# Three turns of the identity behind the sums of each step of layer 0's edge loop, from step 19 on

## The chip, the cores and the metric

The kernel runs on one core of one Trainium2 chip. The metric is the device time of one execution in microseconds, from the runs of the program; the median of three runs before the change is 929.86 us (928.89 to 931.95).

## The reference, cut to what matters

A graph of 1,250 nodes with 512 features and 21,250 edges (each edge both ways, and a loop per node, sorted by destination) goes through two layers. In each, every edge makes a message from its source node's row and its own features, and the messages are summed by destination. The part that the change touches is in layer 0:

```python
src, dst = (edge_index[0], edge_index[1])
msg = jax.nn.relu(x[src] + edge_attr @ W_e + b_e)
aggr = jax.ops.segment_sum(msg, dst, num_segments=x.shape[0])
h = (1.0 + eps) * x + aggr
h = jax.nn.silu(_bn(h @ W1 + b1, g1, beta1))
h = h @ W2 + b2
return jax.nn.silu(_bn(h, g2, beta2))
```

Layer 0 is followed by x = layernorm(x + layer 0), and then by layer 1, whose messages are `relu(h[src] @ .. + edge_attr @ .. + b1)` summed in the same way and then put through a gated unit. All is in float32.

## The kernel before, in words

The program is written by hand, engine by engine; each engine has its own list of instructions in program order, and they meet by semaphores only. Nothing reorders them.

Edges come in tiles of 128 (`TILES` = 167, E = 21,250). The edge loop, `edges(L)`, is run once per layer, in steps of two tiles (`STEPS` = 84), numbered j. Twelve tiles make a group with one window of 128 destination nodes; so a window lasts six steps. The parts of a step, by engine:

- GpSimd gathers the source rows of a tile into one of 14 slots by an indirect DMA (`gather`, L479). It waits until the slot's old tile is done with.
- ScalarE copies the gathered rows of odd tiles into a PSUM bank (`place`, L895), so that TensorE adds onto them; it makes the high half of each message (relu, L939), and the high half of the features of each chunk of four tiles (L895).
- VectorE adds the product to the gathered rows for even tiles (`add_product`, L1170), makes the low half of a message (L1162; not for every fourth tile, which is kept whole), the low features (L1085), and the one-hot matrices that say which destination an edge has (L1156).
- TensorE makes the edge products of the step's two tiles (`edge_product`, L577, two products a tile in layer 0, three in layer 1), and then the sums of the two tiles of two steps ago (`sum_product`): one-hot times message, as a high and a low product (L607, L608) or, for the whole tile, in one line that is two passes (L605).
- SyncE loads the features, four tiles at a time.

When a group's last sums are in, ScalarE copies the window's sums out of PSUM (`copy_window`, L895 with tile `sums`), in step last + 2; TensorE turns them with four transposes (`turn_window`, L630), at the end of step last + 3; VectorE adds them to the nodes' rows (`add_window`, L1185).

TensorE's order within a step is that of the code: edge products, sums, then `turn_x` (L643) in steps 3 to 12 of layer 0, then `turn_window` where a group ends. `turn_x` puts x, four transposes per block of 128 nodes, into bank 7 (`start_bank`), from where ScalarE starts the sums. In step 14 TensorE counts, in the same bank, the edges that lie outside their window (L655), and in step 16 VectorE makes a flag of the count (`left_flag`) and tells it by `flag_ready`. From there on bank 7 is not used in layer 0.

`keep_busy(turns)` (L557) transposes the identity so many times; it stands before the edge loops and around the steps between the two layers, not in the edge loop.

Of the kernel before, what the change touches and what calls it, by code (L numbers as in the profile page):

```python
# [11 lines left out]
P = 128  # L12
# [14 lines left out]
STEPS = -(-TILES // 2)  # L27
BLOCKS = -(-N // P)
# [9 lines left out]
TURN_X = 3  # L38
# [11 lines left out]

LAST_PIECES = [(0, P), (P, 3 * P), (4 * P, 3 * P), (7 * P, N - 7 * P)]
HEAD = 2
KA = KD - 1

COLS = {}
# [22 lines left out]
def gnn_program(nc, x, src, dst, attr0, attr1, W_e, b_e, W1, W2, V1h, V1e, v_b1, V2, v_b2, Wg, cols, out):  # L78
    with ExitStack() as ctx:
# [16 lines left out]
        def keep(name, width, dt=F32, parts=P):  # L96
            t = at(name, [parts, width], dt, small[0])
            small[0] += -(-width * 4 // 64) * 64
            assert small[0] <= A0, name
            return t  # L100
# [7 lines left out]
        ident = keep("ident", P)  # L108
# [119 lines left out]
        start_bank = bank[7]  # L228
# [9 lines left out]
        left_ready, left_counted, flag_ready = map(sem, ("left_ready", "left_counted", "flag_ready"))  # L238
# [73 lines left out]
        def step_tiles(j):  # L312

            return range(2 * j, min(TILES, 2 * j + 2))
# [6 lines left out]
        def last_step(g):  # L321

            return (min(TILES, (g + 1) * GROUP) - 1) // 2
# [220 lines left out]
        def _(pe):  # L544
# [9 lines left out]
            def keep_busy(turns):  # L554

                for _ in range(turns):
                    nc.tensor.transpose(bank[3][:, 0:P], ident[:, :], ident[:, :])  # L557

            def edge_product(L, t):

                i, c, ks = t // 2, t // CHUNK, slice(t % CHUNK * P, (t % CHUNK + 1) * P)
                if t % CHUNK == 0:
                    pe.wait_ge(attr_split[L], c + 1)
                if odd(t):

                    pe.wait_ge(placed[L], i + 1)
                else:

                    wait(pe, added[L], i - ADD_BANKS + 1)
                if L == 0:  # L570

                    passes = [(attr_1[:, c % RING, ks], We_hi[:, :]), (attr_hl[:, c % RING, ks], We_lh[:, :])]
                else:
                    hi, lo = attr_hi[:, c % RING, ks], attr_lo[:, c % RING, ks]
                    passes = [(hi, V1e_hi[:, :]), (hi, V1e_lo[:, :]), (lo, V1e_hi[:, :])]
                for n, (features, W) in enumerate(passes):
                    mm = nc.tensor.matmul(edge_bank(t), features, W, start=n == 0 and not odd(t),  # L577
                                          stop=n == len(passes) - 1, skip_group_check=odd(t))
                mm.then_inc(add_mm[L], 1)

            def prime(L):

                anything = (We_hi[0:1, :], x1_hi[0:1, 0, 0:D])[L]
                for b in place_bank:
                    mm = nc.tensor.matmul(b, ones_row[:, :], anything, start=True, stop=True)
                mm.then_inc(primed[L], 1)
                if L == 0:
                    keep_busy(12)

            def sum_product(L, t):  # L590

                g, c = t // GROUP, t // CHUNK
                start, stop = t % GROUP == 0, t % GROUP == GROUP - 1 or t == TILES - 1
                if whole(L, t):
                    pe.wait_ge(relued[L], t + 1)
                else:
                    pe.wait_ge(low[L], lows(L, t + 1))
                if t % CHUNK == 0:
                    pe.wait_ge(hot_ready[L], c + 1)
                if start:  # L600

                    wait(pe, window_added[L], g - 1)
                acc, h = sum_bank[g % 2], hot[L][:, c % HOT, t % CHUNK, :]
                if whole(L, t):
                    mm = nc.tensor.matmul(acc, h.bitcast(F32), msg_whole[:, t % MSG, :], start=start, stop=stop)  # L605
                else:
                    nc.tensor.matmul(acc, h, msg_hi[L][:, t % MSG, :], start=start, stop=False)  # L607
                    mm = nc.tensor.matmul(acc, h, msg_lo[L][:, t % MSG, :], start=False, stop=stop)  # L608
                if L == 1 and t == chunk_tiles(c).stop - 1:
                    mm = degrees(c)  # L610
                mm.then_inc(summed[L], 1)
# [13 lines left out]
            def turn_window(L, g):  # L625


                pe.wait_ge(window_copied[L], g + 1)
                for k in range(KD):
                    tr = nc.tensor.transpose(sum_bank[g % 2][:, k * P:(k + 1) * P], sums[L][:, g % 2, k * P:(k + 1) * P],  # L630
                                             ident[:, :])
                tr.then_inc(window_turned[L], 1)

            def turn_x(b):

                pe.wait_ge(x_in_done[b // XB], 16)
                if b == 0:
                    pe.wait_ge(base_copied, 1)
                else:

                    pe.wait_ge(agg_start, b)
                for k in range(KD):
                    tr = nc.tensor.transpose(start_bank[:, k * P:(k + 1) * P], x_in[:, b, k * P:(k + 1) * P], ident[:, :])  # L643
                tr.then_inc(x_turned, 1)

            def edges(L):
                prime(L)
                for j in range(STEPS + SUM_LAG + TURN_AFTER):
                    if j < STEPS:
                        for t in step_tiles(j):  # L650
                            edge_product(L, t)
                    if L == 0 and j == TURN_X + BLOCKS + 1:
                        pe.wait_ge(left_ready, 1)
                        pe.wait_ge(agg_start, BLOCKS)
                        nc.tensor.matmul(misc[0:1, 16:17], left_n[:, 0:1], ones[:, 0:1], start=True,  # L655
                                         stop=True).then_inc(left_counted, 1)
                    if 0 <= j - SUM_LAG < STEPS:
                        for t in step_tiles(j - SUM_LAG):
                            sum_product(L, t)
                    if L == 0 and 0 <= j - TURN_X < BLOCKS:  # L660
                        turn_x(j - TURN_X)
                    for g in range(GROUPS):
                        if last_step(g) + SUM_LAG + TURN_AFTER == j:
                            turn_window(L, g)
# [42 lines left out]
            keep_busy(24)  # L707
            pe.wait_ge(we_split, 1)
            edges(0)
            keep_busy(20)  # L710
            leftover(0)
# [34 lines left out]
            def turn_y(t, ks):  # L746

                r = rows_in(t)
                for k in ks:
                    tr = nc.tensor.transpose(bank[t % 2][0:r, k * P:(k + 1) * P], y_t[:, k, t * P:t * P + r], ident[:, :])  # L750
                return tr


            pe.wait_ge(silu_done, KH + KD - 1)
            for t in range(HEAD):
                turn_y(t, range(KA)).then_inc(head_turned, 1)
            pe.wait_ge(mlp_out, 3 * (KH + KD))
            keep_busy(16)
            for t in range(BLOCKS + 3):
                if t < BLOCKS:  # L760
                    for i, (at_node, _) in enumerate(LAST_PIECES):
                        if t == at_node // P:

                            pe.wait_ge(silu_done, KH + KD + i)
                    if t < HEAD:

                        pe.wait_ge(head_added, t + 1)
                        turn_y(t, [KA]).then_inc(back_turned, 1)
                        keep_busy(8)
# [28 lines left out]

            pe.wait_ge(v1e_split, 1)
            edges(1)  # L800
            leftover(1)

# [271 lines left out]
        def _(dve):  # L1074
# [259 lines left out]
            def head_add(t, cols):  # L1334

                if cols.start == 0:
                    if t == 0:
                        dve.wait_ge(rows_in_done, 32)
                    dve.wait_ge(head_turned, t + 1)
                else:  # L1340
                    dve.wait_ge(back_turned, t + 1)
                return nc.vector.tensor_tensor(lnx[:, t, cols], bank[t][:, cols], rows[:, t, cols], ALU.add)
# [4 lines left out]
            for c in range(KH + KD):  # L1347
# [9 lines left out]
                if c == KH + KD - 1:  # L1357

                    head_add(0, slice(0, KA * P)).then_inc(head_added, 1)
                if c + W1_FIRST < KH:  # L1360
# [47 lines left out]

            early, late = slice(0, KA * P), slice(KA * P, D)
            for t in range(BLOCKS + 3):  # L1410
                if t < HEAD:

# [192 lines left out]
```

## Time and profile before

| what | value |
|---|---|
| median of three runs | 929.86 us (928.89 to 931.95) |
| the profiled execution's own time | 934.32 us |
| its span, first to last instruction | 932.5 us |
| its mean granted TensorE clock | 0.938 |
| busy share of TensorE, VectorE, ScalarE, GpSimd | 88%, 69%, 48%, 39% |
| layer 0's edge loop, about | 14 to 278 us |
| layer 1's edge loop, about | 439 to 725 us |

Times in the profile are from the span's start. PE is TensorE's matmuls (transposes too), PEld its weight loads, DVE is VectorE, ACT ScalarE, POOL GpSimd. A line such as L577 is a line of the kernel before. PEclk is the granted clock: 1.00 is 2.4 GHz and 0.50 is 1.2 GHz. A wait is put down to whoever ended it: "issue" is a wait that nothing in the profile explains, "remote" one that was ended by a source that the profile can't name. The starts of matmuls are recorded; their ends are modelled, so durations of neighbours overlap, and the distance from start to start is the better measure.

### The profile page before, as it was taken

What the parts mean: (1) busy time and instruction counts of PE and PEld (TensorE: products, weight loads), DVE (VectorE), ACT (ScalarE), POOL (GpSimd) and SP (SyncE); (2) the same over time, 40 slices, a digit from 0 to 9 for tenths busy, and PEclk for the clock granted to TensorE, in tenths of its full rate; (3) what the DMA queues carried; (4) which work ended last, traced back from release to release, by engine and by line L of the source; (5) the groups of instructions that cost most, each with busy time, mean ns of one, the idle gap of its engine ahead of it and who ended that gap; (6) DMA issues with size and microseconds to landing.
All of it is one profiled execution on the core that took longest, in us unless ns stands there. A gap on an engine that the chain in (4) does not pass through costs nothing.

```text
span 932.5 us, 11516 instructions
## 1 busy us (share of the span) xinstructions
PE 820.9 (88%) x3754; PEld 666.7 (71%) x3754; DVE 639.3 (69%) x1138; ACT 452.1 (48%) x810; POOL 362.4 (39%) x379
## 2 busy tenths in 40 slices
PE   7797868888799999997678989989789999999996
PEld 6464645555568999875467767767668889898995
DVE  6687757777698954396377868878689666354345
ACT  4696756776676422211365656656556321111122
POOL 6576656666620000024656656656552000000001
PEclk9899888889899999999789999989989999999998
DMA  8988776577640050015757766667652111010011
GB/s 226 289 267 252 226 216 205 179 215 214 205 146 25 1 181 1 1 46 171 214 157 233 222 208 212 200 198 216 202 180 80 35 69 68 1 68 1 1 46 65
DMA packets 49814, 133.87 MB, mean 144 GB/s; under 512 B 8815, under 2 KB 9071, under 8 KB 49368
## 3 DMA queue, kind: packets, MB, share of 16 engines
q0 software_dynamic: 26560, 87.05, 30.4%
q1 hardware_dynamic: 22700, 45.60, 15.3%
q8 instruction: 31, 0.51, 0.2%
q10 hardware_dynamic: 492, 0.45, 0.2%
q14 instruction: 31, 0.25, 0.1%
HBM read 127.95 MB, written 5.12 MB: 143 GB/s over the span
## 4 chain that ended last, share of the span: by engine, by line
PE 64%; DVE 17%; issue 7%; another core or an unknown queue 7%; ACT 2%; DMA 1%; DVEq 0%; ACTq 0%; POOL 0%; POOLq 0%
PE banks L550 35%; PE banks L577 14%; DVE msg_lo L1162 6%; PE banks L607 5%; DVE raw L1170 5%; PE banks L608 4%; PE banks L605 2%; PE banks L630 2%; PE banks L621 1%; DVE hot L1156 1%; DVE attr_hl L1085 1%; DVE agg L1185 1%; DVE attr_lo L1085 1%; DVE stats L1298 1%
## 5 line engine op out<-in xcount | busy, mean ns | idle before, releaser
L479 POOL DMA_INDIRECT raw<-table_dram,src_sb x166 | 166.7, 1004 | 108.0 <-DVE msg_lo L1162 57.6
L479 POOL DMA_INDIRECT raw<-in_x,src_sb x166 | 168.0, 1012 | 93.3 <-issue 46.1
L1170 DVE TENSOR_TENSOR raw<-banks,raw 128x512 f32<-128x512 f32 x168 | 115.4, 687 | 116.8 <-remote 71.5
L939 ACT ACTIVATE msg_hi<-raw 128x512 fp32r<-128x512 f32 x168 | 105.8, 630 | 130.9 <-DVE raw L1170 83.3
L607 PE MATMUL banks<-msg_hi,hot 128*128 128x512 f32 x293 | 126.5, 432 | 35.4 <-DVE msg_lo L1162 32.2
L501 POOL TENSOR_TENSOR moments<-moments,minus_half 128x1 f32<-128x1 f32 x32 | 20.2, 630 | 306.0 <-DVE moments L1304 280.4
L608 PE MATMUL banks<-msg_lo,hot 128*128 128x512 f32 x293 | 120.3, 411 | 0.0
L1162 DVE SCALAR_TENSOR_TENSOR msg_lo<-raw,msg_hi 128x512 fp32r<-128x512 f32 x168 | 114.6, 682 | 0.0
L895 ACT ACTIVATE banks<-raw 128x512 f32<-128x512 f32 x166 | 98.7, 595 | 18.1 <-DMA raw<-table_dram,src_sb 11.6
L607 PEld LDWEIGHTS banks<-msg_hi,hot 128*128 128x128 f32 x293 | 58.6, 200 | 65.2 <-DVE msg_lo L1162 47.7
L577 PE MATMUL banks<-We_hi,attr 97*128 97x512 f32 x167 | 91.6, 548 | 3.5 <-issue 2.8
L1162 DVE SCALAR_TENSOR_TENSOR msg_lo<-banks,msg_hi 128x512 fp32r<-128x512 f32 x125 | 85.3, 683 | 0.0
L577 PE MATMUL banks<-V1e_hi,attr_hi 128*128 128x512 f32 x167 | 73.9, 442 | 9.2 <-ACT banks L895 6.7
L939 ACT ACTIVATE msg_hi<-banks 128x512 fp32r<-128x512 f32 x125 | 72.9, 583 | 8.6 <-remote 6.4
L577 PE MATMUL banks<-We_lh,attr_hl 128*128 128x512 f32 x167 | 71.6, 429 | 0.0
L577 PE MATMUL banks<-V1e_lo,attr_hi 128*128 128x512 f32 x167 | 69.5, 416 | 0.0
L577 PE MATMUL banks<-V1e_hi,attr_lo 128*128 128x512 f32 x167 | 69.3, 415 | 0.0
L608 PEld LDWEIGHTS banks<-msg_lo,hot 128*128 128x128 f32 x293 | 58.8, 201 | 11.2
L1156 DVE TENSOR_TENSOR hot<-iota_f,in_window 128x512 fp32r<-128x512 f32 x84 | 56.9, 678 | 0.0
L630 PE MATMUL banks<-ident,sums 128*128 128x128 f32 x112 | 22.3, 333 | 36.5 <-issue 19.9
L577 PEld LDWEIGHTS banks<-We_hi,attr 97*128 97x128 f32 x167 | 35.2, 211 | 25.9 <-issue 17.5
L550 PE MATMUL banks<-x_hi,Wg_hi 128*128 128x512 f32 (+2 forms) x144 | 50.7, 352 | 0.5 <-issue 0.5
(169 smaller groups left out, 1772.6 us busy)
## 6 DMA issues: line engine op xcount, KB each, us to landing
attr_sb<-in_attr SPq DMA_DIRECT2D x84, 128.0 KB
attr_sb<-in_attr SPq DMA_DIRECT2D x42, 256.0 KB
Wg_raw<-in_Wg SPq DMA_DIRECT2D x3, 1536.0 KB, 6.3
raw<-in_x,src_sb POOLq DMA_INDIRECT x166
raw<-table_dram,src_sb POOLq DMA_INDIRECT x166
x_in<-in_x SPq DMA_DIRECT2D x5, 512.0 KB
rows<-in_x SPq DMA_DIRECT2D x1, 2560.0 KB, 12.2
table_dram<-table_sb SPq DMA_DIRECT2D x9, 256.0 KB, 2.0
```

What stands on the lines that cost most here:

```text
L479: pool.indirect_dma_start(rows_of(L, t), None, tables[L], bass.IndirectOffsetOnAxis(ap=src_sb[:, t:t + 1], axis=0)).then_inc(gathered[t % ...
L501: nc.gpsimd.tensor_tensor(moments[:, slot * 4 + 2:slot * 4 + 3], moments[:, slot * 4 + 1:slot * 4 + 2], minus_half[:, 0:1], ALU.pow).then_ ...
L550: mm = nc.tensor.matmul(acc, a, b, start=start and i == 0, stop=stop and i == len(passes) - 1)
L577: mm = nc.tensor.matmul(edge_bank(t), features, W, start=n == 0 and not odd(t), stop=n == len(passes) - 1, skip_group_check=odd(t))
L607: nc.tensor.matmul(acc, h, msg_hi[L][:, t % MSG, :], start=start, stop=False)
L608: mm = nc.tensor.matmul(acc, h, msg_lo[L][:, t % MSG, :], start=False, stop=stop)
L630: tr = nc.tensor.transpose(sum_bank[g % 2][:, k * P:(k + 1) * P], sums[L][:, g % 2, k * P:(k + 1) * P], ident[:, :])
L895: return nc.scalar.activation(to, of, ACT.Copy)
L939: nc.scalar.activation(to[:, t % MSG, :], edge_bank(t) if odd(t) else rows_of(L, t), ACT.Relu).then_inc(relued[L], 1)
L1156: nc.vector.tensor_tensor(hot[L][:, c % HOT, 0:len(tiles), :], nodes, own, ALU.is_equal).then_inc(hot_ready[L], 1)
L1162: nc.vector.scalar_tensor_tensor(msg_lo[L][:, t % MSG, :], edge_bank(t) if odd(t) else rows_of(L, t), 0.0, msg_hi[L][:, t % MSG, :].bitcas ...
L1170: nc.vector.tensor_tensor(rows_of(L, t), edge_bank(t), rows_of(L, t), ALU.add).then_inc(added[L], 1)
```

## The change

Behind the sums of each step of layer 0 with TURN_X + BLOCKS + 5 < j < STEPS, that is 18 < j < 84, so steps 19 to 83, TensorE waits for `flag_ready` and transposes the identity three times into the first 128 columns of bank 7. Nobody reads them.

```diff
--- before.py
+++ after.py
@@ -50,6 +50,7 @@
 
 LAST_PIECES = [(0, P), (P, 3 * P), (4 * P, 3 * P), (7 * P, N - 7 * P)]
 HEAD = 2
+FILL = 3
 KA = KD - 1
 
 COLS = {}
@@ -659,6 +660,10 @@
                             sum_product(L, t)
                     if L == 0 and 0 <= j - TURN_X < BLOCKS:
                         turn_x(j - TURN_X)
+                    if L == 0 and TURN_X + BLOCKS + 5 < j < STEPS:
+                        pe.wait_ge(flag_ready, 1)
+                        for _ in range(FILL):
+                            nc.tensor.transpose(start_bank[:, 0:P], ident[:, :], ident[:, :])
                     for g in range(GROUPS):
                         if last_step(g) + SUM_LAG + TURN_AFTER == j:
                             turn_window(L, g)
```

On TensorE the order changes at each step's end. Here is step 20, which ends with the turn of a window, as it stood in the kernel before (L577 are the edge products, L607 and L608 the sums, L630 the turn of the window; `sums_104` is ScalarE's copy of it, `hot_102` the one-hots):

```order
L577 MATMUL banks<-We_hi,attr_111 128x512 [waits added0,attr_split0]
L577 MATMUL banks<-We_lh,attr_hl 128x512
L577 MATMUL banks<-We_hi,attr_111 128x512 [waits placed0]
L577 MATMUL banks<-We_lh,attr_hl 128x512
L607 MATMUL banks<-msg_hi_97,hot_102 128x512 [waits window_added0,hot_ready0,low0]
L608 MATMUL banks<-msg_lo_100,hot_102 128x512
L607 MATMUL banks<-msg_hi_97,hot_102 128x512 [waits low0]
L608 MATMUL banks<-msg_lo_100,hot_102 128x512
L630 MATMUL banks<-ident,sums_104 128x128 [waits window_copied0]
L630 MATMUL banks<-ident,sums_104 128x128 x3
```

And step 20 in the changed kernel, where the lines have a number higher by one:

```order
L578 MATMUL banks<-We_hi,attr_111 128x512 [waits added0,attr_split0]
L578 MATMUL banks<-We_lh,attr_hl 128x512
L578 MATMUL banks<-We_hi,attr_111 128x512 [waits placed0]
L578 MATMUL banks<-We_lh,attr_hl 128x512
L608 MATMUL banks<-msg_hi_97,hot_102 128x512 [waits window_added0,hot_ready0,low0]
L609 MATMUL banks<-msg_lo_100,hot_102 128x512
L608 MATMUL banks<-msg_hi_97,hot_102 128x512 [waits low0]
L609 MATMUL banks<-msg_lo_100,hot_102 128x512
L666 MATMUL banks<-ident 128x128 [waits flag_ready]
L666 MATMUL banks<-ident 128x128 x2
L631 MATMUL banks<-ident,sums_104 128x128 [waits window_copied0]
L631 MATMUL banks<-ident,sums_104 128x128 x3
```

Three transposes of the identity (L666) stand behind the step's sums and ahead of the turn of the window. In a step without a turn they are its last instructions. Nothing else moved, on this engine or another.

## Rows read from the trace of the kernel before

**Rows 1.** The page: busy time of the engines, and the chain that ended last.

```profile
PE 820.9 (88%) x3754; PEld 666.7 (71%) x3754; DVE 639.3 (69%) x1138; ACT 452.1 (48%) x810; POOL 362.4 (39%) x379
...
PE 64%; DVE 17%; issue 7%; another core or an unknown queue 7%; ACT 2%; DMA 1%; DVEq 0%; ACTq 0%; POOL 0%; POOLq 0%
```

**Rows 2.** Table by stretches: us, busy us (count) of each engine, PEclk, DMA share, GB/s.

```profile
34.00:70.71 36.71, 33.91 (x149) 23.53 (x147) 30.41 (x52) 32.63 (x63) 25.80 (x25) 0.98 0.87 272
76.39:268.77 192.38, 158.75 (x541) 108.44 (x540) 144.03 (x229) 136.28 (x261) 119.27 (x119) 0.88 0.69 206
520.45:711.84 191.39, 167.23 (x750) 132.54 (x748) 151.34 (x257) 117.76 (x216) 116.30 (x116) 0.94 0.65 200
101.73:105.36 3.63, 3.63 (x11) 2.53 (x9) 3.48 (x6) 1.95 (x5) 1.68 (x2) 0.50 0.20 65
108.51:112.65 4.14, 4.14 (x18) 3.03 (x17) 4.08 (x8) 3.71 (x8) 3.17 (x3) 1.00 0.79 234
```

**Rows 3.** Groups by form, TensorE: late part of layer 0; then layer 1; then early part.

```profile
L577 PE MATMUL banks<-We_hi,attr 97*128 97x512 f32 x124 | 70.1, 565 | 0.9 <-ACT banks L895 0.5 <-issue 0.3
...
L630 PE MATMUL banks<-ident,sums 128*128 128x128 f32 x44 | 9.8, 362 | 19.0 <-issue 15.0 <-ACT sums L895 4.0
...
L577 PE MATMUL banks<-V1e_hi,attr_hi 128*128 128x512 f32 x119 | 51.7, 434 | 0.0
...
L643 PE MATMUL banks<-ident,x_in 128*128 128x128 f32 x34 | 5.4, 282 | 0.2 <-issue 0.2
L630 PE MATMUL banks<-ident,sums 128*128 128x128 f32 x8 | 1.3, 279 | 0.4 <-issue 0.4
```

**Rows 4.** Timeline of TensorE, a smooth stretch: start us, us, what [idle before].

```profile
108.51 0.40 PE L577 MATMUL banks<-We_hi,attr 97*128 97x512 f32 x1
108.74 0.40 PE L577 MATMUL banks<-We_lh,attr_hl 128*128 128x512 f32 x1
...
112.65 0.40 PE L577 MATMUL banks<-We_hi,attr 97*128 97x512 f32 x1
```

**Rows 5.** Timeline of TensorE, the turn of a window and the step behind it.

```profile
116.55 0.40 PE L608 MATMUL banks<-msg_lo,hot 128*128 128x512 f32 x1
120.89 1.12 PE L630 MATMUL banks<-ident,sums 128*128 128x128 f32 x4 [3.94 <-issue]
...
122.24 0.63 PE L577 MATMUL banks<-We_lh,attr_hl 128*128 128x512 f32 x1
122.66 0.63 PE L577 MATMUL banks<-We_hi,attr 97*128 97x512 f32 x1
```

**Rows 6.** Timeline of ScalarE at the same turn.

```profile
120.24 0.60 ACT L895 ACTIVATE sums<-banks 128x512 f32<-128x512 f32 x1 [4.03 <-remote]
```

**Rows 7.** Who waited for whom, late part of layer 0: us, times, longest.

```profile
DVE raw L1170 <- remote: 30.5, 8, 4.8
...
ACT sums L895 <- remote: 18.5, 6, 4.0
```

**Rows 8.** Timeline of TensorE in the early part: a step with four transposes.

```profile
37.42 0.48 PE L577 MATMUL banks<-We_hi,attr 97*128 97x512 f32 x1
...
39.38 0.60 PE L643 MATMUL banks<-ident,x_in 128*128 128x128 f32 x4
39.73 0.48 PE L577 MATMUL banks<-We_hi,attr 97*128 97x512 f32 x1
```

**Rows 9.** Timeline of TensorE at the kernel's start, at the lower clock.

```profile
11.38 2.56 PE L557 MATMUL banks<-ident 128*128 128x128 f32 x12
```

**Rows 10.** Timeline of TensorE in layer 1: the first products of two pairs of steps.

```profile
643.16 0.39 PE L577 MATMUL banks<-V1e_hi,attr_hi 128*128 128x512 f32 x1
...
648.14 0.39 PE L577 MATMUL banks<-V1e_hi,attr_hi 128*128 128x512 f32 x1
```

**Rows 11.** Timeline of GpSimd in the late part of layer 0: one gather.

```profile
115.52 0.95 POOL L479 DMA_INDIRECT raw<-in_x,src_sb  x1 [0.30 <-issue]
```

**Rows 12.** Who waited for whom, layer 1: us, times, longest.

```profile
ACT sums L895 <- remote: 18.4, 5, 5.0
```

## The prediction

> **What bounds the kernel now.** Start with the page. TensorE is busy for 88% of the span and heads the chain of work that ended last with 64% [rows 1]. The change touches only the edge loop of layer 0, from step 19 on, so the shares of the whole span say little; I cut that stretch out. The table by stretches has three rows [rows 2]: the early part of layer 0 (34.00 to 70.71 us), its late part (76.39 to 268.77), and most of layer 1's edge loop (520.45 to 711.84). In the late part the mean granted clock is 0.88, against 0.98 and 0.94 in the others, and VectorE, ScalarE and GpSimd are busy for 75, 71 and 62% of it: nothing is full on average. The groups by form count 124 first products there, two per step, so 62 steps in 192.38 us, **3.10 us a step** [rows 3].
>
> The timeline of TensorE shows what a step is when nothing stands still. From 108.51 to 112.65 its instructions start 0.23 to 0.24 us apart without a gap, two steps in 4.14 us [rows 4]: 2.07 us a step. So in a smooth stretch TensorE itself is on the path. VectorE is close behind: it is busy for 4.08 of those 4.14 us [rows 2]. Eleven turns of a window (44 transposes [rows 3]) add 0.43 us each (priced below), 0.08 a step. The smooth step is then 2.15 us, and 3.10 less 2.15 leaves **0.95 us a step, 59 us in all, that is lost**.
>
> Where it is lost: TensorE's timeline at the turn of a window [rows 5]. It ends its sums at 116.95 and stands still until 120.89; ScalarE, whose copy of the window it waits for, is itself released after 4.03 us, by a source that the profile can't name ("remote") [rows 6]. Such standstills come about once a window: ScalarE's copy alone waited 18.5 us in 6 of them, VectorE's add 30.5 us in 8, up to 4.8 at a time [rows 7]. After each the clock stands at 0.50: the stretch from 101.73 to 105.36 is one step of 3.63 us, all of it TensorE's [rows 2]. So two losses: the standstill and the slow clock behind it. The mean clock of 0.88 over 192.38 us means 23 us of full-speed cycles missing, or 46 us at the lower level (1.2 GHz), some of them in standstills. Half of 46 us, 23 us, is the most that a clock held at 2.4 GHz could give back.
>
> **The change, part by part.** It adds three transposes of the identity, with their loads, behind the sums of steps 19 to 83: 65 steps, 195 transposes. It removes and moves nothing. No engine waits for them and their bank is free by then.
>
> *The wait* on the flag adds no time: VectorE sets it in step 16, three steps earlier, and it stays set. Behind it are only TensorE's own instructions.
>
> *One transpose, full clock.* TensorE already does almost this: in the early part each step ends with four transposes of x. Its step from 37.42 to 39.73 takes 2.31 us, and eight products at 0.235 would take 1.88, so four transposes cost 0.43: 0.35 from the first of them (39.38) to the next product (39.73), and 0.08 that the first product behind transposes takes longer [rows 8]. Three cost 0.35 x 3/4 + 0.08: **0.345 us a step**.
>
> *At the lower level:* twelve turns of the identity at the kernel's start take 2.56 us, 0.213 each, against 0.35 / 4 = 0.088 above [rows 9]; three take 0.64 us. With 46 us at that level and some 3.3 us to a slow step, about 14 steps pay 0.30 us more: 4 us.
>
> *Sum with all losses as they are:* 65 x 0.345 = 22.4, plus 4, less what falls into a standstill. In a turning step the three transposes stand behind the sums and ahead of the turn, where TensorE waits anyway: 11 x 0.345 = 4 us covered. That is **+22 us**, the upper bound.
>
> *What the losses do.* The trace has no row for this stage with fill in it, so I bound it by the two other stretches. Layer 1: 119 first products, 59 steps in 191.39 us [rows 3], 3.24 a step; its smooth pace is 4.98 us for two steps (643.16 to 648.14) [rows 10], with the turns 2.57; lost: 0.67. The early part: 13 steps (counted by their first products) in 36.7 us, 2.82 each; 42 transposes make ten and a half sets of four, 0.35 a step, so smooth 2.42; lost: 0.40. A step that gives TensorE more to do loses less. One reason is in the rows: GpSimd starts a gather every 1.25 us while it is not held (0.95 and 0.30 between two) [rows 11], 2.50 us for a step's two, so a TensorE at 2.07 runs faster than rows are fetched, and one at 2.5 doesn't. With the fill the smooth step is 2.15 + 0.345 = 2.50 us. By layer 1's losses it would be 3.17 in all: 0.07 more than now, **+4 us** over 65 steps. Layer 1 is nearest in pace, the stage's own losses are nearest in everything else (copies, adds, loads); I take the middle, **+13 us**, since the losses plainly don't vanish at a pace of 2.57.
>
> The sum is made against the profiled execution, 934.32 us (span 932.5): 947. The median of the runs is 929.86, 4.5 lower, so the forecast against it is **943 us**. A measurement of this kernel can tell about 0.3%, 2.8 us, from no change.
>
> **The rivals.**
>
> *A: the fill takes the standstills away (faster).* Place: the waits of ScalarE's copy and VectorE's add in steps 19 to 74. For it: the early part has four transposes in most steps, a clock of 0.98, and no standstill of that kind; it lost only 0.40 a step. Price: 2.50 + 0.40 = 2.90 us, 0.20 less than now, 65 x 0.20 = 13 us: 917. It decides once a standstill falls from some 4 us to under about 2.5. Against it: layer 1 goes at 2.57 and still has ScalarE's copy waiting 18.4 us in 5 [rows 12]; and in the early part ScalarE had the turned x to copy as well, which the fill doesn't give it.
>
> *B: only the clock is kept up (no difference).* The drops follow standstills of 3 to 4 us. If the added columns held the clock at 2.4 GHz behind them, the 14 slow steps would each give back some 1.3 us (3.3 us against 2.07), 18 in all, and the fill would cost 18 (22 less the 4 for slow steps): 930, with 925 as the end where all 23 us come back. Against it: the fill is issued ahead of the standstill and is over within 0.35 us, and nothing is in TensorE's queue during the 3.94 us [rows 5]; what the clock falls for is missing there. The Trainium skill, "TensorE: Matmul & The Clock Gate", section "HAM oscillation — how this bites in real kernels", says that waits for data let TensorE drop to its lower clock, once per wait, and that the remedy is to order the work so that it meets no such waits. The trace agrees with the first half: the 3.94 us at 116.95 are followed by products 0.43 us apart [rows 5]. By that rule work added beside the waits helps only so far as it shortens them.
>
> *C: VectorE and ScalarE are set back too (slower still).* A later product delays VectorE's add and the gathers behind it, so each standstill stays and the slow steps lengthen: the 4 us aren't covered, and losses grow by a tenth (6 us): +32, 961.
>
> *D: it does nothing to the path.* If VectorE at 4.08 of 4.14 us were the true bound, 0.345 a step would need slack in TensorE; the rows show none in smooth steps [rows 4]. It can hide only where TensorE waits. I count D with B.
>
> **How the numbers follow.** Forecast (+4 to +22 us): 0.56. A 0.22, B with D 0.14, C 0.08. The range: the forecast's own bounds give 934 to 952; it has to reach past A (917, give or take a few) on the low side and part of C on the high side: **911 to 956**. The likeliest case's own range stands at 934 to 952. Both signs hold weight. Slower by over 0.3%: the forecast and C, 0.61. Within: most of B, 0.13. Faster: A and the rest of B, 0.26.
>
> **What would show it.** Right: the late part of layer 0 grows from 192 to some 205 us, smooth pairs of steps take 4.8 us in place of 4.14, standstills ahead of the turns still number about ten, somewhat shorter, the mean clock stays near 0.88, layer 1 and the dense products keep their length. Wrong: smooth pairs at 4.14 with the transposes in gaps (D); "remote" waits of ScalarE's copy and VectorE's add well under 10 us in all (A); a clock above 0.95 with standstills as long as before (B).

## The result, and the profile after

| | before | changed |
|---|---|---|
| median of 20 runs, us | 930.73 (918.54 to 936.58) | 933.68 (926.01 to 942.59) |
| ratio, 95% interval | | 1.0063 (1.0039 to 1.0087) |
| the profiled execution: its own time / span, us | 934.32 / 932.5 | 930.32 / 928.5 |

The change makes the kernel slower by 0.6%, some 6 us, where 13 were forecast. The medians of all twenty runs lie only 3 us apart; the ratio is that of the faster runs, those within 1.5% of their own kernel's fastest (15 of 20 before, 19 of 20 after). So the sign is clear and the size is not: 3 to 6 us. The two profiled executions happen to lie the other way round by 4 us: single executions of this kernel scatter by more than the effect, so only stretches of the two traces are compared below, and the verdict is that of the runs.

The page of the changed kernel: the span, the engines' busy time, the chain that ended last.

```profile
span 928.5 us, 11906 instructions
...
PE 827.1 (89%) x3949; PEld 678.4 (73%) x3949; DVE 638.7 (69%) x1138; ACT 451.9 (49%) x810; POOL 361.2 (39%) x379
...
PE 67%; DVE 18%; another core or an unknown queue 6%; issue 6%; ACT 1%; DMA 1%; DVEq 0%; ACTq 0%; POOL 0%; POOLq 0%
```

The table by stretches of the changed kernel (us; busy us and count of PE, PEld, DVE, ACT, POOL; PEclk; DMA share; GB/s): the late part, 62 steps as in [rows 2]; one step behind a standstill; two smooth steps.

```profile
72.84:267.94 195.10, 169.83 (x727) 121.64 (x726) 144.54 (x230) 136.37 (x262) 120.69 (x120) 0.92 0.70 209
165.41:169.12 3.71, 3.71 (x14) 2.66 (x12) 3.09 (x5) 2.85 (x7) 2.79 (x4) 0.67 0.71 209
169.12:173.91 4.79, 4.79 (x25) 3.58 (x24) 2.40 (x5) 2.57 (x5) 3.37 (x4) 1.00 0.79 237
```

The same 62 steps took 192.38 us before and take 195.10 now, 3.10 and 3.15 a step. The granted clock rose from 0.88 to 0.92. TensorE's groups by form there:

```profile
L578 PE MATMUL banks<-We_hi,attr 97*128 97x512 f32 x124 | 57.5, 464 | 0.1
...
L608 PE MATMUL banks<-msg_hi,hot 128*128 128x512 f32 x93 | 42.2, 454 | 25.1 <-DVE msg_lo L1167 25.1
...
L666 PE MATMUL banks<-ident 128*128 128x128 f32 x186 | 32.1, 284 | 0.0
...
L631 PE MATMUL banks<-ident,sums 128*128 128x128 f32 x44 | 6.8, 278 | 0.0
```

All 186 turns of those steps are there, and no idle time stands before them. The idle time in front of the turn of a window, 19.0 us before [rows 3], is gone; 25.1 us now stand before the high product of the sums (L608). TensorE's timeline, two smooth steps:

```profile
169.12 0.48 PE L578 MATMUL banks<-We_hi,attr 97*128 97x512 f32 x1
...
170.85 0.39 PE L609 MATMUL banks<-msg_lo,hot 128*128 128x512 f32 x1
171.08 0.49 PE L666 MATMUL banks<-ident 128*128 128x128 f32 x3
171.32 0.48 PE L578 MATMUL banks<-We_hi,attr 97*128 97x512 f32 x1
...
172.81 1.02 PE L606 MATMUL banks<-msg_whole,hot 128*128 128x512 f32 x2
173.67 0.49 PE L666 MATMUL banks<-ident 128*128 128x128 f32 x3
173.91 0.48 PE L578 MATMUL banks<-We_hi,attr 97*128 97x512 f32 x1
```

The first takes 2.20 us, the second, with a whole tile, 2.59: **2.39 us a step**, 2.07 before [rows 4]. So the turns stand on the path at 0.32 us a step, close to the 0.345 worked out. Now a standstill and the slow step behind it, from TensorE's timeline and, last, VectorE's; then who waited for whom in the late part (us, times, longest), the changed kernel and one row of the kernel before:

```profile
155.03 0.60 PE L631 MATMUL banks<-ident,sums 128*128 128x128 f32 x4
...
158.75 0.40 PE L578 MATMUL banks<-We_lh,attr_hl 128*128 128x512 f32 x1
163.04 0.80 PE L608 MATMUL banks<-msg_hi,hot 128*128 128x512 f32 x1 [3.89 <-DVE msg_lo L1167]
...
164.49 0.63 PE L609 MATMUL banks<-msg_lo,hot 128*128 128x512 f32 x1
164.91 0.84 PE L666 MATMUL banks<-ident 128*128 128x128 f32 x3
165.41 0.78 PE L578 MATMUL banks<-We_hi,attr 97*128 97x512 f32 x1
```

```profile
161.10 0.69 DVE L1190 TENSOR_TENSOR agg<-banks,agg 128x512 f32 x1 [5.22 <-remote]
```

```profile
PE banks L608 <- DVE msg_lo L1167: 25.1, 11, 3.9
...
DVE agg L1190 <- remote: 21.0, 5, 5.2
...
DVE raw L1175 <- remote: 7.4, 4, 3.8
```

```profile
DVE agg L1185 <- remote: 8.5, 2, 6.0
```

TensorE waits 3.89 us for a message that VectorE could not begin, because VectorE itself was held, in its add of a window (L1190), by a source that the profile can't name (the last section comes back to it). Such waits of ScalarE and VectorE come to 28.4 us in 9 in the late part, where the kernel before had 57.5 us in 16: the 49.0 of [rows 7] and 8.5 in the add of a window (some of that at the same time). So the turns are paid in full in every step, 62 x 0.32 = 20 us, and the stretch grows by 2.7: most of their price comes back as waits, and slow steps behind them, that don't happen. Smooth pace with the turns of windows 2.39 + 0.07 = 2.46; 3.15 less 2.46 leaves **0.69 us a step lost, 0.95 before**, and layer 1 lost 0.67 at its pace.

### The profile page after: what moved, and what is told of

It reads as the page before. It is cut to its first block, busy times and chain, and to the rows that moved or that the text cites. A ratio compares the mean times of both kernels' runs of the same rounds, so it can differ in the third digit from the quotient of the medians.

```text
span 928.5 us, 11906 instructions
## 1 busy us (share of the span) xinstructions
PE 827.1 (89%) x3949; PEld 678.4 (73%) x3949; DVE 638.7 (69%) x1138; ACT 451.9 (49%) x810; POOL 361.2 (39%) x379
## 3 DMA queue, kind: packets, MB, share of 16 engines
q0 software_dynamic: 26560, 87.05, 30.8%
## 4 chain that ended last, share of the span: by engine, by line
PE 67%; DVE 18%; another core or an unknown queue 6%; issue 6%; ACT 1%; DMA 1%; DVEq 0%; ACTq 0%; POOL 0%; POOLq 0%
PE banks L551 35%; PE banks L578 15%; DVE msg_lo L1167 7%; PE banks L608 5%; DVE raw L1175 5%; PE banks L609 5%; PE banks L606 2%; DVE hot L1161 1%; PE banks L666 1%; PE banks L622 1%; PE banks L631 1%; DVE attr_hl L1090 1%; DVE attr_lo L1090 1%; DVE agg L1190 1%
## 5 line engine op out<-in xcount | busy, mean ns | idle before, releaser
L608 PE MATMUL banks<-msg_hi,hot 128*128 128x512 f32 x293 | 126.3, 431 | 44.4 <-DVE msg_lo L1167 42.3
L608 PEld LDWEIGHTS banks<-msg_hi,hot 128*128 128x128 f32 x293 | 58.7, 200 | 72.6 <-DVE msg_lo L1167 55.4
L578 PE MATMUL banks<-We_hi,attr 97*128 97x512 f32 x167 | 78.2, 468 | 3.1 <-issue 2.9
L578 PE MATMUL banks<-We_lh,attr_hl 128*128 128x512 f32 x167 | 68.7, 412 | 0.0
L551 PE MATMUL banks<-x_hi,Wg_lo 128*128 128x512 f32 (+2 forms) x144 | 50.8, 353 | 0.0
L551 PE MATMUL banks<-x_lo,Wg_hi 128*128 128x512 f32 (+2 forms) x144 | 50.8, 353 | 0.0
```

Source lines behind the costliest of these rows:

```text
L551: mm = nc.tensor.matmul(acc, a, b, start=start and i == 0, stop=stop and i == len(passes) - 1)
```

## Experiments: more turns, and no gathers

A *standstill* is a stretch of some microseconds in which TensorE does nothing; the *smooth pace* is the time of a step without one, with its share of a window's turn. Each set of runs below met one chip, and every kernel in it is compared with the kernel before on the same chip. Theory S: with its standstills the late part of layer 0 is held to some 3.1 us a step by something outside TensorE, and work added to an engine only takes the place of standstills until its own pace reaches that. Theory P, the one of the forecast: the losses shrink only partly as the pace falls. The edits, each one alone; first the number of turns, on the changed kernel:

```diff
-FILL = 3
+FILL = 6
```

and likewise 12. Six turns:

> Six turns a step in place of three; steps 19 to 83 of layer 0 took 200.1 us before and 200.0 us with three. Theory S (those steps are held to about 3.08 us a step by something outside TensorE, of which the standstills are the visible part, so that more work on TensorE only takes their place): the smooth step grows to 2.74 us and the 65 steps still take 200 to 205 us; the whole stays within 0.5% of the kernel with three. Theory P (TensorE's work is paid in full, and the losses per step merely fall with the pace, from 0.95 to about 0.7 us): 65 x 0.345 more, less a little, so the steps take 215 to 222 us and the whole is 1.6 to 2.4% over the kernel before.

Twelve turns:

> Twelve turns a step. The smooth step is 2.07 + 12 x 0.088 + 0.08 + 0.08 for the turn of a window = 3.29 us, over the 3.08 that the steps take on average now. Theory S: TensorE becomes the bound at last, few or no standstills are left, the clock stays full, 65 steps take 214 to 220 us: 1.5 to 2.2% over before. Theory P: losses of 0.4 to 0.7 us a step on top, 240 to 260 us, 4 to 6.5% over before.

Then the gathers of layer 0 from the fifteenth tile on were left out. What layer 0 adds up is then made from what already stands in the fourteen slots; every instruction of the other engines stays. On the kernel before:

```diff
+        told = sem("told")
...
-                before = L * len(range(t % RAW, TILES - 1, RAW))
-                engine.wait_ge(gathered[t % RAW], (before + t // RAW + 1) * 16)
+                if L == 0 and t >= RAW:
+                    engine.wait_ge(told, t - RAW + 1)
+                else:
+                    engine.wait_ge(gathered[t % RAW], (L + t // RAW + 1) * 16)
...
+                if L == 0 and t >= RAW:
+                    nc.gpsimd.nop().then_inc(told, 1)
+                    return
                 pool.indirect_dma_start(rows_of(L, t), None, tables[L],
```

> The kernel before with the gathers of layer 0 from tile 14 on left out (GpSimd only tells that the slot is ready, so its rows are those of an earlier tile). If the standstills come from the gathers (theory S with the gathers as the supply), steps 19 to 83 run at the smooth pace of 2.15 us with the clock at 1.00: 140 us in place of 200, the whole about 870 us, 6% under. If the standstills come from the exchange between the engines itself (sums, copy of the window, turn), they stay, and the steps take 190 to 200 us.

The same on the changed kernel:

> The changed kernel (three turns a step) with the same gathers left out. With the standstills gone nothing covers the turns: 65 x 0.345 = 22 us over the run without gathers and without turns under theory S and under theory P alike, if the smooth step is TensorE's; if VectorE (4.08 of 4.14 us busy) is the bound there, clearly less than 22.

Measured in one set, against a kernel before of 937.18 us:

| kernel | median, us | ratio to before | steps 19 to 80 in its trace, us |
|---|---|---|---|
| six turns | 945.29 | 1.0091 (1.0036 to 1.0147) | 198.29 |
| twelve turns | 961.53 | 1.0278 (1.0220 to 1.0336) | 216.12 |
| no gathers | 884.52 | 0.9443 (0.9380 to 0.9505) | 144.34 |
| no gathers, three turns | 891.54 | 0.9528 (0.9475 to 0.9581) | 153.40 |

Their rows for those 62 steps, in this order, from the tables by stretches:

```profile
75.22:273.51 198.29, 181.27 (x913) 136.39 (x912) 145.69 (x230) 138.26 (x264) 121.23 (x119) 0.98 0.69 204
```

```profile
80.44:296.56 216.12, 214.77 (x1286) 176.58 (x1284) 145.34 (x229) 137.72 (x263) 121.61 (x120) 1.00 0.63 186
```

```profile
64.87:209.21 144.34, 141.88 (x541) 94.69 (x540) 142.41 (x229) 134.46 (x261) 0.00 (x0) 1.00 0.20 57
```

```profile
69.63:223.03 153.40, 153.27 (x728) 115.81 (x726) 145.11 (x230) 135.72 (x263) 0.00 (x0) 1.00 0.18 54
```

Two smooth steps with six turns, then two pairs with twelve:

```profile
132.57:138.01 5.44, 5.44 (x32) 4.25 (x30) 3.09 (x5) 3.59 (x8) 4.22 (x5) 1.00 0.82 246
```

```profile
134.49:141.22 6.73, 6.73 (x43) 5.54 (x41) 5.58 (x9) 5.62 (x12) 4.96 (x5) 1.00 0.62 167
141.22:147.99 6.77, 6.77 (x43) 5.56 (x42) 4.32 (x7) 3.83 (x9) 3.23 (x3) 1.00 0.54 163
```

Six turns give TensorE 0.65 us more a step (5.44 / 2 less 2.07), 40 us over 62 steps, and the stretch is 6 us longer. At twelve turns the clock is 1.00, TensorE is busy for 214.77 of 216.12 us, and it has no standstill of 2 us left; only there is TensorE the bound, at 3.49 us a step. The unnamed waits are not gone even so: VectorE still has 14.7 us of them in 4, up to 4.9 at a time, which no longer reach TensorE.

```profile
DVE raw L1175 <- remote: 8.2, 2, 4.9
```

Theory S is the nearer one between 0 and 6 turns: each lands at 3.10 to 3.20 us a step. Its own figures were low, though. For 65 steps it gave 200 to 205 us with six turns, and the traces make 208; it gave 214 to 220 with twelve, and they make 227. Part of that is the price of a turn: three, six and twelve cost 0.32, 0.65 and 1.31 us a step, 0.11 each in proportion, and not 0.088 each with 0.08 once. Without gathers the standstills are all gone, without any turn: clock 1.00, 2.33 us a step. The exchange between the engines doesn't make them by itself; the gathers are needed. And in that quiet stretch the three turns cost 9.1 us, not 62 x 0.32 = 20: VectorE is busy for 142.41 of 144.34 us, so it is the bound there, and TensorE, at 2.15 with the turns of windows, has room. By the medians of the runs the three turns cost 7.0 us there. The smooth stretch that the forecast read as TensorE's own had VectorE within 2% of it, and over longer stretches VectorE decides.

## Experiments: what of a gather does it, and a delay elsewhere

Narrow gathers, on the kernel before (layer 0 then sums other numbers than the tiles' rows):

```diff
+                w = P if L == 0 and t >= RAW else D
-                pool.indirect_dma_start(rows_of(L, t), None, tables[L],
+                pool.indirect_dma_start(rows_of(L, t)[:, 0:w], None, tables[L] if w == D else x.rearrange("n (a d) -> (n a) d", d=P),
```

> The kernel before, with the gathers of layer 0 from tile 14 on a quarter as wide (128 of 512 columns; what they fetch is not the tile's rows). Each is still one indirect DMA of 128 rows with its descriptors and its sixteen signals, but a quarter of the bytes. Without any gather the 65 steps ran at 2.32 us each, with no standstill. If the bytes (the DMA engines' time) hold the steps to 3.08 us, the standstills go as they did without gathers: about 885 us, 5 to 6% under before. If it is what a gather costs whatever its width (descriptors, signals, GpSimd's 1.25 us each), the standstills stay, about one a window: within 1.5% of before.

No feature loads after the third chunk (the edges' features are then those of the first three chunks), on the kernel before:

```diff
                 wait(sp, attr_split[L], c - RING + 1)
+                if L == 0 and c >= RING:
+                    for h in range(P // parts):
+                        nc.sync.nop().then_inc(attr_in[L][c % RING], 16)
+                    return
```

> The kernel before, with the feature loads of layer 0 from the fourth chunk on left out (SyncE only tells that the chunk is there, so its values are old). The gathers stay whole. If the sum of all DMA traffic makes the standstills, a fifth less of the bytes and a third less of the packets brings them down by a third or more: the whole 1.5 to 4% under before. If it is the gathers alone, nothing changes: within 1% of before.

A delay on VectorE in place of the turns, on the kernel before:

```diff
                             low_message(L, t)
+                    if L == 0 and TURN_X + BLOCKS + 5 < j < STEPS:
+                        for _ in range(2):
+                            link(nc.vector.tensor_copy(lf_hot[0][:, :], iota_f[:, :]))
```

> The kernel before, with two small copies on VectorE in each of steps 19 to 83 in place of TensorE's turns, about 0.2 us each and 0.5 a step with what links them, 30 us of VectorE's time in all. TensorE is given no more columns. Theory S (the steps have room for any delay up to about 3.1 us a step): VectorE's own load rises from 2.3 to 2.8 us a step and the whole grows by 0 to 1.2%, as with the turns, with fewer and shorter standstills. If the small price of the three turns came from a clock that they kept up, this run has nothing of the kind and costs its 30 us, 3% over before.

This set told something else first: **the kernel before took 827.89 us** in it (824.52 to 829.88, 21 runs), 100 less than on any chip until then. Against that: narrow gathers 823.62 us, 0.9944 (0.9925 to 0.9962); no feature loads 828.39, 1.0008 (0.9989 to 1.0028); the delay 848.37, 1.0262 (1.0238 to 1.0286). In its traces the clock stands at or near 1.00 through the whole late part and the unnamed standstills are absent, so the three say nothing about them here. All three were run again; the narrow gathers and the delay then met a chip that has them. The copies' group and the table's row for 62 steps of the delay:

```profile
L1234 DVE COPY lf_hot<-iota_f 128x128 f32<-128x128 f32 x122 | 27.6, 226 | 2.1
```

```profile
67.32:240.80 173.48, 157.72 (x541) 88.14 (x540) 167.39 (x350) 136.41 (x261) 114.88 (x120) 1.00 0.80 235
```

The copies are 27.6 us of VectorE's time, and the kernel paid 20.5 for them.

## Experiments: both kinds of chip

The kernels were run again in three more sets. The first of them met a chip with standstills (before: 932.69 us):

> The kernel before, unchanged, for a trace of it on this chip. In the last set the kernel before took 828 us, in the sets ahead of it 930 to 937: the standstills are not in the program. If this chip is one of the fast ones: no idle stretch of 2 us or more at TensorE in steps 19 to 83, the clock at 1.00, and those steps in 155 to 170 us (GpSimd's two gathers at 1.25 us each, 2.50 a step, being the bound: 162). If it is one of the slow ones: the trace looks as the first did.

> The changed kernel. On a chip without standstills: if GpSimd's 2.50 us a step is the bound, TensorE's 2.48 us with three turns still fit beneath it and the whole is within 0.6% of before (0 to 5 us). If TensorE and VectorE at 2.1 to 2.3 us are the bound there, the turns cost 10 to 22 us, 1.2 to 2.7%. On a chip with standstills: again 0.3 to 1% over before.

> Six turns, smooth step 2.72 + 0.08 us. On a chip without standstills nothing is left that could pay for it: 65 x (2.80 - 2.50) = 20 us over before if GpSimd's pace is the bound there, 2.4%, and 30 us or more if it is not. On a chip with standstills: about 1%, as before.

> The kernel before without the gathers of layer 0 from tile 14 on. On a chip without standstills it can only take away GpSimd's pace: 65 x (2.50 - 2.32) = 12 us less, 1.4% under before, in place of the 5.6% that it took away on the slow chip. On a chip with standstills: 5 to 6% under again.

Measured: unchanged 929.45 us, 1.0034 (0.9988 to 1.0080); three turns 932.94, 1.0050 (1.0011 to 1.0090); six turns 930.91, 1.0045 (1.0012 to 1.0078); no gathers 876.42, 0.9464 (0.9401 to 0.9526). Three and six turns can't be told apart, and hardly from no change: the unchanged kernel's own ratio reaches 1.0080, and the medians of all runs with three turns and before, 932.94 and 932.69, are the same.

The next met one with standstills too (before: 929.86 us):

> The kernel before, unchanged, for its trace on this chip. Where the runs of before are near 828 us: steps 19 to 83 in 155 to 170 us, no idle stretch of 2 us at TensorE, the clock at 1.00, layer 1's edge loop shorter by some 50 us too. Where they are near 930: as the first trace, 195 to 202 us.

> The changed kernel. Where before is near 828 us: 0 to 5 us over it if GpSimd's 2.50 us a step is the bound there, 10 to 22 us if TensorE and VectorE are. Where before is near 930 us: 0.3 to 0.8% over it, the third time.

> The kernel before with gathers of 128 columns in place of 512 in layer 0 from tile 14 on. Where before is near 930 us: if the bytes make the standstills, 5 to 6% under before, as without gathers; if what each gather costs whatever its width makes them, within 1.5%. Where before is near 828 us: 0.3 to 1% under before, as it was.

> The kernel before with two small copies more on VectorE in steps 19 to 83, 0.3 us a step or more. They cost 20 us, 2.6%, on the chip without standstills. Where before is near 930 us: 0 to 1% if any delay is taken up by the standstills, whichever engine has it; 2 to 2.6% if only TensorE's own work is.

Measured: unchanged 930.29 us, 1.0002 (0.9969 to 1.0036); three turns 937.67, 1.0104 (1.0054 to 1.0153); narrow gathers 927.17, 0.9941 (0.9900 to 0.9983); the delay 938.13, 1.0101 (1.0043 to 1.0159). Three turns cost more here than the 0.3 to 0.8% expected. The late part in all traces of chips with standstills:

| kernel | 62 steps, us | unnamed waits of ScalarE and VectorE, us (times) | TensorE idle for 2 us or more, times |
|---|---|---|---|
| unchanged | 192.38, 194.65, 196.49 | 57.5 (16), 61.1 (20), 56.4 (17) | 8, 10, 9 |
| three turns | 195.10, 199.12, 202.51 | 28.4 (9), 27.9 (8), 33.1 (8) | 5, 6, 8 |
| six turns | 198.29, 200.15 | 20.3 (9), 23.0 (10) | 3, 3 |
| twelve turns | 216.12 | 14.7 (4) | 0 |
| delay on VectorE | 200.53 | 39.1 (14) | 8 |
| narrow gathers | 190.10 | 36.5 (16) | 7 |

So the sum isn't quite constant: 3.10 to 3.17 us a step without turns, 3.15 to 3.27 with three, 3.20 and 3.23 with six. Narrow gathers in the table by stretches, and VectorE's unnamed wait there:

```profile
70.72:260.82 190.10, 157.24 (x541) 106.53 (x540) 144.28 (x229) 136.49 (x261) 119.34 (x120) 0.89 0.30 85
```

```profile
DVE raw L1171 <- remote: 19.8, 9, 4.7
```

A quarter of the gathers' bytes, DMA share down from 0.69 to 0.30, and VectorE's add still waits 19.8 us in 9 for the unnamed source, at a clock of 0.89; the kernel gains 0.6% (0.2 to 1.0), as on the chip without standstills. The packets fell too, from 80 to 32 a gather by the page's counts (26,560 in all before, 19,264 with 152 of 332 gathers narrow). The unnamed waits are as many as before and a third shorter in all (36.5 us in 16 against 56.4 in 17 on this chip), so bytes or packets have a part in it, but a small one in the time: 6 us of the 50 that go without gathers. The rest is something that a gather brings with it at either width. The delay on VectorE, 2.6% where there are no standstills, costs 1.0% here:

```profile
73.36:273.89 200.53, 164.71 (x541) 97.09 (x540) 167.36 (x350) 137.60 (x261) 114.96 (x120) 0.93 0.69 203
```

So about half of a delay on VectorE is taken up: 9 us are paid (4 to 15) in place of 20.5. Here TensorE was given no work that could hold its clock up, and the clock is still 0.93, against 0.87 for the unchanged kernel on this chip. The last set met a chip without standstills again (before: 827.56 us):

> The changed kernel. Where before is near 828 us, its steps take about 2.6 us each (163.6 us for 63 steps in the run without feature loads there), and TensorE with three turns needs 2.48: 0 to 5 us over before if the gathers' pace leaves room, up to 10 us, as in the pair without gathers, if it does not. Where before is near 930 us: 0.3 to 1% over it, as three times already.

> The kernel before, for its trace on this chip. Near 828 us: no standstills, steps 19 to 83 in about 165 us, layer 1's edge loop some 50 us shorter. Near 930 us: as the first trace.

> The kernel before without the feature loads of layer 0 from the fourth chunk on. Where before is near 930 us: narrow gathers took away 0.6% there, so bytes don't count; if every DMA's descriptors and signals count, the loads (two in two steps, beside four gathers) are a third of them and 1.5 to 2.5% go; if it is the gathers alone, within 0.5%. Where before is near 828 us: within 0.3%, as it was.

Measured: three turns 832.43 us, 1.0067 (1.0040 to 1.0094); unchanged 827.58, 1.0008 (0.9987 to 1.0029); no feature loads 828.64, 1.0009 (0.9990 to 1.0028). Rows for 62 steps: unchanged (and below it 59 steps of layer 1's loop, those of [rows 2]), three turns, no feature loads.

```profile
65.70:221.70 156.00, 141.96 (x541) 94.34 (x540) 145.66 (x230) 136.44 (x261) 119.17 (x120) 1.00 0.90 262
453.04:604.77 151.73, 151.73 (x749) 127.66 (x748) 151.18 (x257) 118.32 (x218) 114.49 (x118) 1.00 0.82 255
```

```profile
67.03:227.41 160.38, 157.27 (x728) 114.23 (x726) 146.46 (x230) 136.61 (x261) 123.03 (x120) 1.00 0.86 254
```

```profile
62.54:223.45 160.91, 145.20 (x541) 93.14 (x540) 146.07 (x230) 136.49 (x261) 123.23 (x122) 1.00 0.71 204
```

Without standstills the unchanged kernel takes 2.52 us a step, which is GpSimd's pace, as its timeline shows (gathers 1.25 us apart), and the gathers are what ScalarE waits for there:

```profile
98.58 0.95 POOL L479 DMA_INDIRECT raw<-in_x,src_sb  x1 [0.30 <-issue]
99.84 0.95 POOL L479 DMA_INDIRECT raw<-in_x,src_sb  x1 [0.30 <-issue]
```

```profile
ACT banks L895 <- DMA raw<-in_x,src_sb: 18.5, 23, 1.6
```

With three turns it takes 2.59 us, 4.4 us more over 62 steps; the whole grows by 4.9. (One trace's stretch is not that sharp: without feature loads it is 160.91, 4.9 more, and the whole is unchanged.)

This bears on what was said above. Three turns cost 4.9 us where there are no standstills, and 5 to 10, by the ratios of three sets, where there are: no less. With three turns the pace of the gathers alone would take up most of the price, so that the shrinking standstills are needed for it can't be told from these runs. It can be with more work. By the pace of 2.52, six turns would cost 65 x (2.79 - 2.52) = 18 us and twelve 65 x (3.45 - 2.52) = 60 (estimates, not run on such a chip); with standstills they cost 4 to 9 and 24 to 26. The delay on VectorE was run on both: 20.5 and 9 us. Layer 1's 59 steps, 191.39 us in the first trace, take 151.73, at a clock of 1.00 and with TensorE never idle: 2.57 us a step, exactly its smooth pace. Of the 102 us between the chips, 36 lie in layer 0's late part and 40 in those steps of layer 1.

## Why the forecast was right in direction and at least twice too large

- *What bounds the stretch.* The standstills and the slow clock behind them were read rightly as the loss; 0.95 us a step of it was there, but not all of it is standstills: a chip without any still takes 2.52 us a step, 0.37 over the smooth 2.15, at the gathers' pace. That the smooth step is TensorE's own was half right. VectorE is within 2% of it, and without gathers VectorE decides: three turns then cost 9 us where the sum had 20. On a chip without standstills GpSimd's 2.50 decides, and they cost 5.
- *The price of the turns.* 0.345 us a step was forecast; smooth steps grew by 0.32, and a pair of them took 4.79 us, 4.8 forecast. The flag's wait cost nothing. This term held, though its make did not: the cost is in proportion, 0.11 a turn.
- *The cover in turning steps.* 4 us were said to be hidden ahead of a turn, at all eleven turns; only seven of them had a wait ahead of them before. The idle time ahead of the turn did go, all 19 us of it, but because the standstills moved and thinned out, not by 0.345 us each.
- *What the losses do* is the step that failed. It gave +4 us by layer 1's losses and +22 by unchanged losses, and took the middle, 13, "since the losses plainly don't vanish at a pace of 2.57". They fell to 0.69, layer 1's figure almost to the hundredth, which makes +2.9 us over 65 steps in the traces; the runs say 6 (3.6 to 8.1). The upper bound's reason, that the stage's own losses are nearest in everything else, says nothing of how they change with the pace, so it should not have pulled the value up. The late part was to grow from 192 to 205 us at a clock of 0.88; it grew to 195, at 0.92. The forecast's own rows lay on both sides of 2.50, the early part at 2.42 with 0.40 and layer 1 at 2.57 with 0.67; that the second was hit so closely is in part luck. In its place the runs showed that the losses shrink by nearly all that the pace grows: they were 0.95, 0.69, 0.41 and 0.04 us a step at smooth paces of 2.15, 2.46, 2.79 and 3.45 (0, 3, 6, 12 turns). The sum stays at 3.10 to 3.20 in these traces, up to 3.27 in the others, until the pace itself passes it. Three stretches at 2.15, 2.42 and 2.57 stood in the forecast with sums of 3.10, 2.82 and 3.24. The longest two lie close together at paces far apart, which is what such a floor under the sum looks like; the early part lies under it and isn't explained by it. What sets it, and why at 3.1 to 3.3, stays open.
- *Rival A* had the mechanism, fewer standstills, but they shrank by what was added and by no more; that takes the price back and gives no gain. Its sign came true without its price: the unnamed waits of ScalarE's copy and VectorE's add fell to 7.4 us, while 21.0 stood at VectorE's add of a window, where the sign didn't look. *Rival B*: the clock did rise, to 0.92, 0.98 and 1.00 with 3, 6 and 12 turns. It rose as the standstills became fewer, and with the delay on VectorE, which gives TensorE no work, it rose too, 0.87 to 0.93. The Trainium skill's rule on the clock, one drop for each wait for data, weighed in the forecast ("TensorE: Matmul & The Clock Gate", "HAM oscillation — how this bites in real kernels"), is borne out in this: in the changed kernel's late part each of TensorE's five idle stretches of 3.4 to 3.9 us has a slow stretch with it, there is no other, and there is none in the traces without standstills. *C* didn't happen. *D* fell: the smooth steps did lengthen.

## What to carry to other kernels

Where a stretch of the trace is a row of smooth steps and standstills, work out how long both are together, and see whether other stretches of other make come to the same sum: if so, lengthening the smooth steps moves the time little until they pass that sum (shortening them was not tried). A price taken from smooth steps of one engine is then an upper bound; here even the chips without standstills paid a quarter of it, because another engine's pace lay just above. And before such a stretch is tuned at all, the same kernel should be run on another chip: here its largest loss, 100 us of 930, was there in some sets and not in others.

## What was not expected of the hardware

- The same program takes 828 us on some chips (single runs 824.5 to 831.5) and 930 on others (918 to 947). Each chip was met once, so that it is the chip, and not what was going on around it at that time, is likely but not shown. The gap is standstills of 2 to 5 us in both edge loops, and the lower clock behind them.
- The standstills need the gathers (5.6% and 5.4% went with them) but hardly their bytes or packets (0.6% went with three quarters of the bytes). Whether it is their signals or the rate at which GpSimd issues them was not tried. Whether the feature loads have a part is open as well: both runs without them met chips without standstills.
- The unnamed source is a late signal of TensorE. The traces record when each signal arrives. In the standstill shown, the turn of the window ended at 155.63 us, TensorE ran on through a whole step, and the turn's signal is recorded at 160.97; VectorE's add began at 161.10. Over all signals recorded between 72 and 268 us of the span, 68 of TensorE's 184 came over 1 us behind the instruction's end (up to 6.7) in the kernel before, 76 of 190 with three turns, 29 of 174 with twelve, and none of 282 without gathers, nor of 278 in the unchanged kernel on a chip without standstills. VectorE's and ScalarE's came within 0.01 us in every one of these traces. (TensorE's ends are modelled, and where there are standstills a part of the signals isn't in the record.) Why TensorE's signals alone are late, why only beside gathers, and why only on some chips stays open.
